# Three of a sort group's eight steps hand three value columns to GpSimd, and the bucket one-hots are made two steps sooner

## The chip, the cores and the metric

The kernel runs on one core of one Trainium2 chip. The metric is the device time of one execution in microseconds; the engines are TensorE (PE in the profile), VectorE (DVE), ScalarE (ACT), GpSimd (POOL) and SyncE (SP). A program is built once and the same inputs are used in every run.

## The reference

A session recommender on a graph. The part that this change concerns is the first line below: 150,000 weighted edges in random order are summed into 12,501 nodes of 128 features, twice.

```python
h = emb; acc = emb                                  # N = 12501 nodes, D = 128
for _ in range(2):
    h = segment_sum(adj_val[:, None] * h[adj_col], adj_row, num_segments=N)
    acc = acc + h
graph_item_embs = acc / 3
combined = graph_item_embs[items] + item_features[items]      # 512 sessions of 50 items
...                                                 # attention over a session, 12 * l2norm -> select
scores = select @ l2norm(graph_item_embs).T         # (512, 12501)
```

## The kernel before

**Stages.** The kernel first counts how many edges fall into each of 49 buckets of 256 rows (to about 88 us of the profile), then sorts all edges by bucket into a table in HBM (to about 737 us), then goes through the sorted edges twice, with one gather by GpSimd for 128 edges at a time (L649), and last computes the sessions and the scores. Only the sort is touched by the change.

**A sort group.** Edges lie as 128 partitions by 1,172 columns. `GR` = 19 groups have `SG` = 8 steps of `C` = 8 columns each; the last has `LAST` = 3 steps. Every edge has a place (partition, column) in a 128 x 72 picture of its group (`LC` = 72). In a step, DVE makes two one-hots from the places: `hot_columns` (L964, bf16, 128 x 576, into one of `Q` = 4 slots of `hot_c`) and `hot_partitions` (L972, f32, 128 x 1024, into one of four slots of `at_p`). Both read the row of candidates from PSUM and the places from SBUF. The one-hot of the columns is then multiplied by each edge's code and by its value, giving `at_c`, 8 columns t of 2 x 72: ACT does columns 0 to `CA` - 1 = 5 with two activations each (L723, in `payloads`), DVE does the last two in one instruction (`last_columns`, L980, 128 x 288). PE multiplies `at_p` by `at_c` column by column (L1550, in `permute`) and sums the group's picture in a PSUM bank. A slot is used again four steps later.

**After a group.** In step 1 of the next group, after two columns of its own, ACT copies the picture out of PSUM (`evacuate`, L709). GpSimd then does a small gate operation (L598), adds the picture's blocks to the sorted table with 9 indirect DMAs that it issues itself (`scatter`, L604), waits for them to land, and frees the buffers with another gate operation (L611). Then it waits for the next group.

**Places of the next group.** Between its one-hots, DVE works out the places of group g + 1 while group g is permuted: `hot_buckets` (L900, 128 x 3136 bf16, the one-hot of the buckets into the single buffer `hot_b`; the first `KEPT` = 7 groups kept theirs from the counting and need none), PE's prefix sums of it (`edges_before`, L1535 on PE, then the reduction L988 on DVE in step 3), a scan over 1,666 elements (`lane_scan`, L1020) in step 4, six folds (L1037, L1045, L1048) in steps 5 to 7, and in step 7 `place_rounded` (L1054), `place_partition` (L1060) and `place_column` (L1065). Each of these waits for the one ahead of it by the semaphore `s_rk`. The first `hot_columns` of group g + 1 waits for the last of them.

**Order.** The order on each engine is written out by hand, and each engine waits for the others by semaphores alone: `hot_columns` waits until ACT is done with the slot, `hot_partitions` until PE is, ACT waits for `hot_columns` and for PE's release of the slot.

```python
for s in range(SG):                     # sort_group on DVE, cut to what matters
    if s == 0 and hot is hot_b:
        hot_buckets(g + 1)
    ...
    hot_columns(g, s, h); hot_partitions(g, s, h)
    ...                                 # the s-th piece of the places of g + 1
    last_columns(g, s)
```

## Time and profile before

| | |
|---|---|
| median of three runs | 3988.06 us (3985.89 to 3988.77) |
| the profiled execution: its time, its span | 3990.2 us, 3988.2 us |
| DVE busy in the span | 3011.5 us (76%) |
| POOL busy | 2657.9 us (67%) |
| PE busy | 2638.1 us (66%) |
| ACT busy | 830.1 us (21%) |
| L980, DVE's multiplication of the last two columns | x147, 97.7 us, 664 ns each |
| L972, DVE's one-hot of the partitions | x147, 178.6 us, 1215 ns each |
| L723, ACT's activations | x1764, 569.7 us, 415 ns each |
| L900, the bucket one-hots | x12, from 295.9 to 660.3 us |

A busy time is the sum of an engine's instructions; where one starts before the last has ended, both are counted in a mean duration, so the step from start to start is shorter than the mean. The whole span has stages with different limits: the shares above say little on the sort, which lies between about 88 and 737 us. The stage behind it begins with GpSimd's first gather (L649).

### The profile page before, as it was taken

The numbers are of one execution on the slowest core, as the hardware profiler recorded it, in microseconds if no ns is written. First come the engines' busy times: TensorE is split into PE (matmuls) and PEld (weight loads), VectorE is DVE, ScalarE is ACT, GpSimd is POOL, SyncE is SP. The second block draws the span as 40 slices with busy tenths as digits, with TensorE's granted clock in tenths as the row PEclk, the third lists the DMA queues.
The fourth block names the chain that finished last, engine by engine and source line by source line (L and its number), as shares of the span: only waits on it lengthen the run. The fifth ranks groups of instructions, "written<-read, shape, count | busy, mean of one in ns | idle before, by whom it ended". The sixth has DMA issues, their size and how long they took to land.

```text
span 3988.2 us, 79764 instructions
## 1 busy us (share of the span) xinstructions
PE 2638.1 (66%) x14097; PEld 2222.1 (56%) x14098; DVE 3011.5 (76%) x7238; ACT 830.1 (21%) x2728; POOL 2657.9 (67%) x2685
## 2 busy tenths in 40 slices
PE   4899889555566566566666556665556555565898
PEld 2676666455565555555555555555555555553454
DVE  8999999767777677777777677767677777677675
ACT  0999999200000000000000000000000000004554
POOL 1355555777777777777776777777777777775771
PEclk7899999777777776777778677778787787786999
DMA  1011111422222222222223222222222222234343
GB/s 37 3 4 3 3 3 3 110 53 54 55 54 54 54 55 55 55 55 55 55 55 103 62 55 55 56 56 56 56 55 55 55 55 55 54 81 140 95 139 139
DMA packets 165449, 228.71 MB, mean 57 GB/s; under 512 B 79020, under 2 KB 119084, under 8 KB 164908
## 3 DMA queue, kind: packets, MB, share of 16 engines
q0 software_dynamic: 102640, 162.39, 19.8%
q1 hardware_dynamic: 47856, 58.94, 4.8%
q10 hardware_dynamic: 14540, 3.70, 0.8%
q14 instruction: 377, 3.09, 0.2%
q8 instruction: 36, 0.59, 0.1%
HBM read 183.57 MB, written 41.35 MB: 56 GB/s over the span
## 4 chain that ended last, share of the span: by engine, by line
DMA 30%; POOL 27%; issue 19%; DVE 13%; PE 6%; ACT 2%; SPq 2%; ACTq 0%; DVEq 0%; POOLq 0%
POOL store L649 25%; DMA store<-in_L_rec_emb,store 16%; DMA store<-table,store 13%; PE bank L1707 2%; DVE store L1020 2%; DVE big L964 2%; PE bank L1650 2%; POOL store L676 1%; DVE store L972 1%; ACT big L723 1%; DVE big L980 1%; DVE big L1445 1%; SPq L496 1%; DVE store L1045 1%; DVE store L906 1%
## 5 line engine op out<-in xcount | busy, mean ns | idle before, releaser
L1650 PE MATMUL bank<-store,shared 128*128 x9792 | 1731.2, 351 | 1137.5 <-POOLq L634 790.5
L1650 PEld LDWEIGHTS bank<-store,shared 128*128 128x128 f32 x9792 | 1610.9, 258 | 1257.8 <-issue 1255.5
L1338 DVE TENSOR_TENSOR acc<-acc,bank 128x256 f32 x2448 | 1022.6, 418 | 799.7 <-PE bank L1650 780.5
L1288 DVE TENSOR_SCALAR shared<-bank,mlo,mval 128x256 f32<-128x256 f32 x2448 | 1324.0, 541 | 0.0
L649 POOL DMA_INDIRECT store<-in_L_rec_emb,store x1128 | 1065.4, 945 | 384.2 <-issue 326.0
L649 POOL DMA_INDIRECT store<-table,store x1128 | 1066.4, 945 | 370.0 <-issue 317.9
L739 ACT COPY mlo<-store 128x24 f32 (+1 forms) x102 | 21.5, 211 | 2793.0 <-PE bank L1650 1977.6
L723 ACT ACTIVATE big<-big 128x72 f32<-128x72 bf16 x1764 | 569.7, 415 | 0.0
L1550 PE MATMUL bank<-big,store 128*128 128x144 f32 x2352 | 480.2, 333 | 72.1 <-DVE store L972 17.3
L1550 PEld LDWEIGHTS bank<-big,store 128*128 128x128 f32 x2352 | 357.0, 206 | 192.8 <-ACT big L723 169.5
L604 POOL DMA_INDIRECT sorted_edges<-moved,block_to x167 | 311.2, 1863 | 57.1 <-issue 57.1
L676 POOL DMA_INDIRECT store<-combined,sidi x200 | 192.3, 962 | 94.4 <-issue 57.3
L972 DVE TENSOR_TENSOR store<-bank,place_p 128x1024 f32<-128x1024 f32 x147 | 178.6, 1215 | 0.0
L598 POOL TENSOR_TENSOR gate<-gate 128x1 f32<-128x1 f32 x19 | 6.2, 326 | 245.9 <-ACT moved L709 245.9
L964 DVE TENSOR_TENSOR big<-bank,place_c 128x576 bf16<-128x576 f32 x147 | 110.3, 750 | 0.3
L1707 PE MATMUL bank<-acc,big 128*128 128x512 f32 (+1 forms) x200 | 96.5, 625 | 2.6 <-DVE big L1493 2.6
L980 DVE TENSOR_TENSOR big<-big 128x288 f32<-128x288 bf16 x147 | 97.7, 664 | 0.0
L1499 DVE COPY store<-bank 128x512 f32<-128x512 f32 x48 | 33.2, 692 | 65.7 <-PE bank L1707 65.7
L1707 PEld LDWEIGHTS bank<-acc,big 128*128 128x128 f32 x200 | 37.0, 198 | 60.5 <-issue 26.4
L1020 DVE TENSOR_TENSOR_SCAN store<-shared,big 128x1666 int16<-128x1666 bf16 x19 | 68.9, 3629 | 0.7
L1696 PEld LDWEIGHTS bank<-w2c,big 128*128 128x128 f32 x400 | 50.6, 191 | 30.6 <-ACT big L841 18.0
L1419 DVE SCALAR_TENSOR_TENSOR big<-store,maskn,big 128x128 f32<-128x128 f32 x192 | 54.9, 346 | 13.0 <-DMA store<-combined,sidi 12.3
(265 smaller groups left out, 1439.4 us busy)
## 6 DMA issues: line engine op xcount, KB each, us to landing
store<-in_L_rec_emb ACTq DMA_DIRECT2D x3008, 0.5 KB
store<-in_L_rec_emb SPq DMA_DIRECT2D x3008, 0.5 KB
store<-table SPq DMA_DIRECT2D x3008, 0.5 KB
store<-table ACTq DMA_DIRECT2D x3008, 0.5 KB
scores<-store SPq DMA_DIRECT2D x48, 512.0 KB, 2.8
store<-in_L_rec_emb,store POOLq DMA_INDIRECT x1128
store<-table,store POOLq DMA_INDIRECT x1128
table<-acc SPq DMA_DIRECT2D x7, 896.0 KB, 10.6
```

The source lines that it names most:

```text
L604: pool.indirect_dma_start(slots, bass.IndirectOffsetOnAxis(block_to[:, h, k:k + 1], 0), moved[:, h, (skip + k) * R:(skip + k + 1) * R, :]. ...
L649: pool.indirect_dma_start(msg[:, j % RING, :], None, source, bass.IndirectOffsetOnAxis(m_col[:, j:j + 1], 0)).then_inc(s_g[gi % (T // GRP4 ...
L676: pool.indirect_dma_start(seq[:, half, l, :], None, combined, bass.IndirectOffsetOnAxis(sidi[:, l, bt:bt + 1], 0)).then_inc(s_sq[half * NG ...
L723: last = act.activation(at_c[:, r, t, q, :], hot_c[:, r, :, t], ACT.Copy, scale=what[:, bass.ds(n * C + t, 1)])
L964: dve.tensor_tensor(hot_c[:, r, :, :], row_c.unsqueeze(2).broadcast_to([P, LC, C]), place_c[:, h, s * C:(s + 1) * C].unsqueeze(1).broadcas ...
L972: dve.tensor_tensor(at_p[:, r, :, :], row_p.unsqueeze(1).broadcast_to([P, C, P]), place_p[:, h, s * C:(s + 1) * C].unsqueeze(2).broadcast_ ...
L1020: dve.tensor_tensor_scan(summed[:, :, :].rearrange("p b t -> p (b t)"), carry[:, :, :].rearrange("p b t -> p (b t)"), pairs[:, :, :].rearr ...
L1288: dve.tensor_scalar(onehot[:, u % SR, :], bank[7][:, 0:BUCKET], mlo[:, u:u + 1], mval[:, u:u + 1], ALU.is_equal, ALU.mult).then_inc(s_S[u ...
L1338: add = dve.tensor_tensor(acc[:, bass.ds(off, BUCKET)], acc[:, bass.ds(off, BUCKET)], bank[u % PR][:, 0:BUCKET], ALU.add)
L1550: last = pe.matmul(group_bank(h)[:, 0:2 * LC], at_p[:, r, t, :], at_c[:, r, t, :, :].rearrange("p w c -> p (w c)"), start=(s == 0 and t == ...
L1650: last = pe.matmul(bank[u % PR][:, q * D:(q + 1) * D], onehot[:, u % SR, q * P:(q + 1) * P], msg_flat[:, bass.ds(offs[u], D)], start=True, ...
L1707: pe.matmul(score_bank(bt, n)[:, 0:w], selT[:, :], acc[:, 512 * n:512 * n + w], start=True, stop=True).then_inc(s_sc, 1)
```

## The change

In the steps s = 0, 1 and 7 of a group (`LENT`), ACT multiplies five columns instead of six, DVE none instead of two, and GpSimd multiplies columns 5 to 7 in one instruction of 128 x 432 elements, with a semaphore of its own (`s_valg`). On GpSimd the instruction for step 7 of group g + 1 stands behind the DMA issues of `scatter(g)` and ahead of the wait for their landing, and those for steps 0 and 1 of group g + 2 behind it. `hot_buckets` for group g + 2 is now made in step 6 of group g, where before it stood in step 0 of group g + 1, and PE's `edges_before` follows it. PE waits for `s_valg` ahead of column 5 of those steps, and DVE waits for it before it writes the same slot of `hot_c` four steps later.

```diff
+            def last_columns(g, s):                       # on GpSimd
+                n, r = SG * g + s, s % Q
+                pool.wait_ge(s_hc, n + 1)
+                pool.wait_ge(s_pm, n + 1)
+                pool.tensor_tensor(at_c[:, r, CL:C, :, :],
+                                   hot_c[:, r, :, CL:C].rearrange("p n t -> p t n").unsqueeze(2).broadcast_to([P, C - CL, 2, LC]),
+                                   pays[:, bass.ds(n * C + CL, C - CL), :].unsqueeze(3).broadcast_to([P, C - CL, 2, LC]),
+                                   ALU.mult).then_inc(s_valg, 1)
...
+                if ahead:
+                    last_columns(g + 1, SG - 1)
                 pool.wait_ge(s_free, g + 3)
                 pool.wait_ge(s_sct, 16 * (NK * g + blocks))
                 pool.tensor_tensor(gate[:, 2:3], gate[:, 1:2], gate[:, 1:2], ALU.add).then_inc(s_free, 1)
+                if ahead:
+                    last_columns(g + 2, 0)
+                    last_columns(g + 2, 1)
...
-                for t in range(CA):
+                own = CL if s in LENT else CA             # ACT: 5 or 6 columns
+                for t in range(own):
...
                 dve.wait_ge(s_val, CA * n + CA)
+                if (s - Q) % SG in LENT:
+                    ge(dve, s_valg, NL * g + (LENT.index((s - Q) % SG) + 1 - (NL if s < Q else 0)))
...
                 for s in range(SG):                       # sort_group on DVE
-                    if s == 0 and hot is hot_b:
-                        hot_buckets(g + 1)
-                    elif s == 3:
+                    if s == 6 and early:
+                        hot_buckets(g + 2)
+                    if s == 3:
...
-                    last_columns(g, s)
+                    if s not in LENT:
+                        last_columns(g, s)
...
                     permute(g, s, h, SG)                  # sort_group on PE
-                    if s == 0:
-                        edges_before(g + 1, hot)
+                    if s == 6 and hot is not None:
+                        edges_before(g + 2, hot)
```

On DVE, at the seam of the groups 16 and 17 (written out behind the loop), the order before runs from step 7's `hot_columns` (L964) over `place_rounded` (L1054) to the `hot_buckets` of group 18 (L900) and steps 0 and 1:

```order
L964 TENSOR_TENSOR big<-bank,place_c 128x576
L972 TENSOR_TENSOR store<-bank,place_p 128x1024
L1054 TENSOR_SCALAR round<-posf 128x64
L980 TENSOR_TENSOR big<-big 128x288
L1060 TENSOR_SCALAR place_p<-round 128x64
L1065 SCALAR_TENSOR_TENSOR place_c<-place_p,posf 128x64
L900 TENSOR_TENSOR store<-shared,big 128x3136
L964 TENSOR_TENSOR big<-bank,place_c 128x576
L972 TENSOR_TENSOR store<-bank,place_p 128x1024
L980 TENSOR_TENSOR big<-big 128x288
L964 TENSOR_TENSOR big<-bank,place_c 128x576
```

At the same seam the changed kernel has this order, with `hot_columns` now at L992, `place_rounded` at L1082, `place_column` at L1093 and `targets` at L1106:

```order
L992 TENSOR_TENSOR big<-bank,place_c 128x576
L1000 TENSOR_TENSOR store<-bank,place_p 128x1024
L1082 TENSOR_SCALAR round<-posf 128x64
L1088 TENSOR_SCALAR place_p<-round 128x64
L1093 SCALAR_TENSOR_TENSOR place_c<-place_p,posf 128x64
L992 TENSOR_TENSOR big<-bank,place_c 128x576
L1000 TENSOR_TENSOR store<-bank,place_p 128x1024
L992 TENSOR_TENSOR big<-bank,place_c 128x576
L1000 TENSOR_TENSOR store<-bank,place_p 128x1024
L1106 TENSOR_TENSOR block_to<-bank,block_id 128x9
```

The multiplications L980 of steps 7, 0 and 1 are gone, and so is the bucket one-hot between `place_column` and the next `hot_columns`; it stands one step earlier, between the second and the third fold:

```order
L1073 TENSOR_TENSOR store<-store 128x768
L926 TENSOR_TENSOR store<-shared,big 128x3136
L1073 TENSOR_TENSOR store<-store 128x384
L992 TENSOR_TENSOR big<-bank,place_c 128x576
L1000 TENSOR_TENSOR store<-bank,place_p 128x1024
```

On GpSimd a group of the changed kernel (the last one that is `ahead`, written out behind the loop) reads as follows; L609 is the multiplication, L602 and L627 the two gates, L618 the scatter's DMAs:

```order
L602 TENSOR_TENSOR gate<-gate 128x1
L618 DMA sorted_edges<-moved,block_to 18816x16 x9
L609 TENSOR_TENSOR big<-big 128x432
L627 TENSOR_TENSOR gate<-gate 128x1
L609 TENSOR_TENSOR big<-big 128x432 x2
L602 TENSOR_TENSOR gate<-gate 128x1
```

Before, nothing stood between a scatter's DMAs and its second gate, nor between that gate and the next group's first.

## Rows read from the trace of the kernel before

**Rows 1.** Busy time by stretch, two sort groups: microseconds, then each engine's.
```profile
core 0: us, PE busy (x) PEld busy (x) DVE busy (x) ACT busy (x) POOL busy (x), PEclk, DMA share, GB/s
239.51:271.82 32.31, 29.36 (x156) 22.04 (x155) 31.05 (x46) 31.34 (x106) 17.40 (x11) 0.95 0.12 3
403.41:436.43 33.02, 29.50 (x152) 22.14 (x151) 32.40 (x48) 31.35 (x106) 18.26 (x11) 0.93 0.12 3
```
**Rows 2.** Who waited for whom, 110 to 304 us: us in total, times, longest.
```profile
ACT idle L717 <- DVE big L964: 7.2, 6, 2.7
DVE ahead L988 <- PE bank L1535: 5.5, 6, 1.0
```
**Rows 3.** Who waited for whom, 337.17 to 668 us.
```profile
ACT idle L717 <- DVE big L964: 16.3, 11, 2.6
```
**Rows 4.** Timeline of DVE, steps 7 and 0: start, us, instruction.
```profile
657.40 0.75 DVE L964 TENSOR_TENSOR big<-bank,place_c 128x576 bf16<-128x576 f32 x1
658.07 1.22 DVE L972 TENSOR_TENSOR store<-bank,place_p 128x1024 f32<-128x1024 f32 x1
659.20 0.18 DVE L1054 TENSOR_SCALAR round<-posf 128x64 f32<-128x64 f32 x1
659.30 0.68 DVE L980 TENSOR_TENSOR big<-big 128x288 f32<-128x288 bf16 x1
659.89 0.19 DVE L1060 TENSOR_SCALAR place_p<-round 128x64 f32<-128x64 f32 x1
660.11 0.22 DVE L1065 SCALAR_TENSOR_TENSOR place_c<-place_p,posf 128x64 bf16<-128x64 f32 x1
660.25 1.78 DVE L900 TENSOR_TENSOR store<-shared,big 128x3136 bf16<-128x3136 bf16 x1
```
**Rows 5.** Timeline of DVE, one group later, at a seam without L900.
```profile
692.95 0.23 DVE L1065 SCALAR_TENSOR_TENSOR place_c<-place_p,posf 128x64 bf16<-128x64 f32 x1
693.26 0.76 DVE L964 TENSOR_TENSOR big<-bank,place_c 128x576 bf16<-128x576 f32 x1
```
**Rows 6.** Timeline of ACT, the last full group: the stall, a step, the last evacuation.
```profile
683.98 0.19 ACT L717 COPY idle<-ones 128x1 f32<-128x1 f32 x1 [1.44 <-DVE big L964]
...
695.90 3.86 ACT L723 ACTIVATE big<-big 128x72 f32<-128x72 bf16 x12
699.67 0.17 ACT L717 COPY idle<-ones 128x1 f32<-128x1 f32 x1
...
701.02 0.26 ACT L709 COPY moved<-bank 128x144 f32<-128x144 f32 x1
```
**Rows 7.** Timeline, places where DVE and POOL instructions meet.
```profile
78.59 0.80 DVE L953 TENSOR_SCALAR big<-big 128x1248 int32<-128x1248 int32 x1
78.75 1.25 POOL L614 IOTA store<- 128x640 f32 x1 [67.52 <-DVE store L951]
79.43 1.23 DVE L954 TENSOR_SCALAR big<-big 128x1248 f32<-128x1248 int32 x1
...
403.35 0.66 DVE L980 TENSOR_TENSOR big<-big 128x288 f32<-128x288 bf16 x1
403.41 0.60 POOL L598 TENSOR_TENSOR gate<-gate 128x1 f32<-128x1 f32 x1 [12.29 <-ACT moved L709]
...
411.55 3.63 DVE L1020 TENSOR_TENSOR_SCAN store<-shared,big 128x1666 int16<-128x1666 bf16 x1
412.31 4.23 POOL L604 DMA_INDIRECT sorted_edges<-moved,block_to  x1 [0.30 <-issue]
```
**Rows 8.** Timeline of POOL at the start: its plain operations by size.
```profile
4.49 0.29 POOL L566 TENSOR_SCALAR_AFFINE_SELECT ident<-ident 128x128 f32<-128x128 f32 x1 [0.16 <-POOL ident L564]
7.42 1.13 POOL L579 IOTA big<- 128x1152 f32 x1
```
**Rows 9.** Timeline of POOL at the end of the sort.
```profile
701.36 0.19 POOL L598 TENSOR_TENSOR gate<-gate 128x1 f32<-128x1 f32 x1 [10.45 <-ACT moved L709]
...
733.46 0.19 POOL L611 TENSOR_TENSOR gate<-gate 128x1 f32<-128x1 f32 x1 [1.45 <-DMA sorted_edges<-moved,block_to]
737.14 1.01 POOL L649 DMA_INDIRECT store<-in_L_rec_emb,store  x1 [3.49 <-DVE store L1267]
```

More of the change, by code:

```diff
@@ L68, in recommender_program @@
     Q = 4
+    CL = CA - 1
+    LENT = (0, 1, SG - 1)
+    NL = len(LENT)
     ECOLS = (GR * SG + Q) * C
@@ L621, in _ @@
             pool.wait_ge(s_zero, 16)
-            with pool.Fori(0, GR // 2) as i:
+            for s in LENT:
+                last_columns(0, s)
+            last_columns(1, 0)
+            last_columns(1, 1)
+            with pool.Fori(0, GR // 2 - 1) as i:
                 for h in range(2):
-                    scatter(2 * i + h, h)
+                    scatter(2 * i + h, h, ahead=True)
+            scatter(GR - 3, 0, ahead=True)
+            scatter(GR - 2, 1)
             scatter(GR - 1, 0, NKL, FIRST)
@@ L724, in payloads @@
                                               scale=what[:, bass.ds(n * C + t, 1)])
-                    last.then_inc(s_val, 1)
+                    last.then_inc(s_val, 1 + CA - own if t == own - 1 else 1)
             with act.Fori(0, GR // 2) as i:
@@ L1078, in targets, with sort_group @@
                 dve.tensor_tensor(block_to[:, h, 0:blocks], bank[7][:, 0:blocks], number[:, :], ALU.add).then_inc(s_to, 1)
-            def sort_group(g, h, width=LC, hot=hot_b):
+            def sort_group(g, h, width=LC, hot=hot_b, early=True):
                 for s in range(SG):
-                    if s == 0 and hot is hot_b:
-                        hot_buckets(g + 1)
-                    elif s == 3:
+                    if s == 6 and early:
+                        hot_buckets(g + 2)
+                    if s == 3:
                         edges_before(g + 1)
@@ L1153, in _ @@
             sort_group(GR - 3, 0)
-            sort_group(GR - 2, 1, LCL)
+            sort_group(GR - 2, 1, LCL, early=False)
             dve.wait_ge(s_lat, 3)
@@ L1159, in _ @@
                 hot_partitions(GR - 1, s, 0)
-                last_columns(GR - 1, s)
+                if s not in LENT:
+                    last_columns(GR - 1, s)
                 if s == 0:
@@ L1544, in permute @@
                 pe.wait_ge(s_hp, n + 1)
+                own = CL if s in LENT else CA
                 for t in range(C):
-                    if t < CA:
+                    if t < own:
                         pe.wait_ge(s_val, Q * CA + CA * n + t + 1)
-                    elif t == CA:
-                        pe.wait_ge(s_valv, n + 1)
+                    elif t == own and s in LENT:
+                        pe.wait_ge(s_valg, NL * g + (LENT.index(s) + 1))
+                    elif t == own:
+                        pe.wait_ge(s_valv, (SG - NL) * g + (s + 1 - sum(x < s for x in LENT)))
                     last = pe.matmul(group_bank(h)[:, 0:2 * LC], at_p[:, r, t, :],
@@ L1567, in _, with sort_group @@
             edges_before(0, kept[:, 0])
[L1569 removed]
+            pe.wait_ge(s_rk, 1)
+            edges_before(1, kept[:, 1])
+            def sort_group(g, h, hot=hot_b):
                 for s in range(SG):
                     permute(g, s, h, SG)
[L1573 to L1574 removed]
+                    if s == 6 and hot is not None:
+                        edges_before(g + 2, hot)
                     elif s == 4:
@@ L1578, in _ @@
             for g in range(KEPT - 1):
-                sort_group(g, g % 2, kept[:, g + 1])
-            with pe.Fori(KEPT // 2, GR // 2) as i:
+                sort_group(g, g % 2, kept[:, g + 2] if g + 2 < KEPT else hot_b)
+            with pe.Fori(KEPT // 2, GR // 2 - 1) as i:
                 for h in range(2):
-                    sort_group(2 * i + h, h, hot_b)
+                    sort_group(2 * i + h, h)
+            sort_group(GR - 3, 0)
+            sort_group(GR - 2, 1, None)
             for s in range(LAST):
```

6 lines of the change are left out of this document (3 added, 3 removed).

## The prediction

> **What bounds the kernel now.** I read the busy times by stretch first, the waits second, the timeline third. A sort group takes 32.3 us early and 33.0 us late; DVE is busy for 31.05 and 32.40 of them, ACT for some 31.35 in both [rows 1]. So two engines are nearly full, and the waits tell which one sets the pace. DVE waits for PE alone, 5.5 us in six early groups, when the prefix sums come late, and for nothing of weight later [rows 2, 3]. ACT waits for DVE once in a group, 16.3 us in eleven waits late [rows 3], 1.44 us in the last full group, where the scan and the first folds hold back step 5's `hot_columns` [rows 6]. A chain through DVE therefore sets the group's time, with ACT some 1.5 us behind, and early on the loop DVE, ACT, PE, DVE adds about 0.9 us. PE is granted 0.93 to 0.95 of its 2.4 GHz here and its weight loads fill 22 of 33 us [rows 1], so it has room. GpSimd is busy for 17 to 18 us and then waits for the next evacuation, up to 12.29 us [rows 1, 7, 9]. The end of the sort hangs on GpSimd: its chain from the last full picture (701.36) to the last gate (733.46) and the first gather (737.14) has fixed length [rows 9]. What the change is worth is how much sooner ACT can evacuate that picture, now at 701.02 [rows 6].
>
> **What is removed.** On DVE, one multiplication is worth its step from start to start, 659.30 to 659.89, 0.59 us [rows 4], not its 0.68. In steps 0 and 1 nothing else changes: 2 x 0.59 = 1.18. In step 7, `place_rounded` was followed after 0.10 us by a multiplication that had no need of it; now `place_partition` follows and must wait for it, which takes 0.22, as between the next two links (659.89 to 660.11) [rows 4]. That leaves 0.69 - 0.22 = 0.47. Together 1.65 us a group, or for groups 0 to 16, 28.0 us, and 1.2 us more in steps 0 and 1 of group 17. From step 5 of group 17 on, ACT is the slower one (its waits stop at 683.98), and there it is its own saving that counts: an activation takes 3.85/12 = 0.32 us [rows 6], and steps 7 and 0 lose two each, 1.3 us. Sum: 30.5 us. Elsewhere ACT's six fewer activations a group (1.9 us) only keep it behind DVE: its work falls to about 29.3, and DVE's to about 31.5 late and 29.7 early. For the early groups I estimate whether a slot can be late: DVE needs some 10 us for any four steps (four times 1.80 for the two one-hots, two or three multiplications, the pieces of the places), while ACT and PE trail by 6 to 9, so none is.
>
> **What is moved.** `hot_buckets` cost 1.71 us of DVE (660.25 to 661.96) wherever it stands. At the seam it also hid the wait of `hot_columns` for `place_column`: without it the step from one to the other is 0.31 us, with it 0.14 [rows 4, 5]. That costs 0.17 in the twelve groups that have it. Between the second and the third fold it hides a wait of the same kind, about 0.13. I put the two at nothing. PE's prefix sums are now made in step 6 for a reduction in step 3 of the next group: the 5.5 us of early waits [rows 2] go altogether. PE has some 3 us of work more between steps 6 and 7 instead of between 0 and 1; the evacuation comes two ACT steps later, so this is covered. On GpSimd the scatter's issues now meet `hot_buckets` in step 6, and one of them will be held as the scan holds one today (4.23 us instead of 1.55) [rows 7]; GpSimd is about 2 us early there and would lose 1.7 of them. The DVE side has a few more semaphore waits, hidden in the queue behind instructions of 0.7 to 1.2 us.
>
> **What is added, and where it collides.** GpSimd's multiplication of 432 elements for each partition stands in no trace. From below: an iota writes 1,152 elements in 1.13 us, 0.98 ns for each, and the operation of one column takes 0.19 [rows 8, 9], so 432 elements take at least 0.6 us. The affine select reads and writes 128 in 0.29 us [rows 8], 0.78 ns for each behind the fixed part. If two inputs and the output were each paid in turn, an element would cost about 0.8 + 0.8 + 1.0 = 2.6 ns and the instruction 1.3 us. From above: DVE itself takes 0.59 us for 288 elements [rows 4], 2 ns each where its plain f32 one-hot takes 1.1, since the columns are picked out of `hot_c` with a stride. Doubling 2.6 in the same way gives 2.4 us. I take 1.4, near the middle sum, with 0.6 and 2.4 as ends. (An estimate apart from the sum: the Trainium skill, GPSIMD Engine Reference, section 3.1, gives about 2.6 cycles of 1.2 GHz an element with two inputs, and section 7 about one more cycle when the step is over 8 bytes. That would be 1.1 and 1.5 us; no row here has such an instruction.)
>
> That time is not on anyone's path as work. PE needs columns 5 to 7 about 3.2 us after `hot_columns`, when ACT is done with its five; GpSimd starts about 0.15 us after `hot_columns` (the gate starts 0.08 after ACT's copy ends at 701.28 [rows 6, 9]). But DVE and GpSimd hold each other up. The rows show both directions [rows 7]: the one-column gate, 0.19 us alone, takes 0.60 and ends at 404.01, with DVE's L980, which reads two tensors in SBUF; an issue starts under the scan and ends 1.4 us after it; and DVE's L954, the same 1,248 elements as L953, takes 1.23 instead of 0.80, since GpSimd's iota runs until 80.00. So the question is which DVE instructions stand beside the multiplications. In steps 0 and 1 they are one-hots and `targets`, which have one operand in PSUM and L972 lasts 1.215 us on the mean of all 147 (table above), most of them beside scatter issues, as in [rows 4], where GpSimd is idle; the first that could be held is the multiplication of step 2, over 2.7 us after the start. In step 7 it is `place_rounded`, SBUF to SBUF, due 1.05 us after `hot_columns` ends (658.15 to 659.20) [rows 4]. GpSimd ends 0.15 + 1.4 = 1.55 after it: DVE is held for 0.5 us, and 0.1 more by GpSimd's gate right behind. 0.6 x 17 groups = 10.2 us given back.
>
> What holds whom is weighed against a rule here. The Trainium skill (SBUF — State Buffer, "Who interferes with whom") says that a DVE instruction with two SBUF inputs contends with GpSimd's reads, one in a two-port mode with all of GpSimd, and one with a single SBUF input outside these modes not at all. By that rule, the gate under L980 agrees (0.60 us), and L954 agrees (1.23). Applied to step 7 it names `place_rounded` or, at the latest, `place_column`, 0.4 us later: the sum would be 0.2 us a group better if only the latter were held. The page says as well that an issue needs only the write side; the scan has two inputs and holds an issue for 2.7 us here, so the measurement decides.
>
> **Sum.** -30.5 - 5.5 + 10.2 = -25.8 us against the profiled execution (3990.2 us; span 3988.2). The median of the plain runs is 2.1 us below that time, so I subtract from it: 3988.1 - 25.8 = **3962 us**.
>
> **The rivals.**
> 1. *No collision.* The multiplication takes up to 0.9 us, or `place_rounded` isn't held. For: GpSimd's plain operations cost 0.98 ns an element [rows 8]. Against: two inputs, a stride, two types. 3988 - 36 = 3952 us.
> 2. *A long multiplication*, 2.4 us, by the stride that costs DVE double. Held for 1.5 + 0.1 us in step 7: 27 us given back, 3979 us.
> 3. *Slower.* GpSimd's multiplication takes over 2.9 us. From 3.0 on, step 7 gives back all the 36 us (2.1 x 17), and from 2.7 on the multiplication of step 1 reaches into step 2, where L980 reads two SBUF tensors and is held as the gate was. At 3.3 us: 2.5 in step 7; step 1's starts late at 4.2 and ends at 7.5, L980 is due at 5.5, 2.0 more; 4.5 x 17 = 77, or 4029 us. Against: 6.6 ns an element is seven times the iota's rate.
> 4. *No change.* The saving is on DVE and ACT, but GpSimd becomes the bound: 17 to 18 us of issues [rows 1], 3.4 of gates and landing, 1.7 of the new hold and three multiplications of 1.4 make 28, and it must also wait for three `hot_columns` in their order. If it reaches step 7's late, PE, the evacuation and the next scatter slip, and 3984 to 3992 us come out, 3988 with the gain just eaten. Against: the sum leaves 3 us a group.
>
> By the rule of two SBUF inputs alone, rival 1 needs a multiplication under 1.3 us.
>
> **How the numbers follow.** Forecast 0.52, rival 1 0.24, rival 2 0.12, rival 3 0.04, rival 4 0.08. The time is the forecast's. The range runs from 3949 (rival 1 with a little over) to 3979 (rival 2), and leaves out rivals 3 and 4 and some of both ends, under 2 in 10. About 0.2% (8 us) is what a measurement can tell from no change. Faster: the first three cases and a bit of rival 4, 0.88. Within 0.2%: 0.07. Slower: 0.05.
>
> **What would show it.** The group falls from 32.3 to about 30.3 us early and from 33.0 to about 32.1 late; the last evacuation stands near 675. GpSimd's 56 multiplications take about 1.4 us. `place_rounded` starts some 1.6 us behind the end of step 7's `hot_columns`, or shows as 0.7 us long. L988 never waits for PE. ACT's wait at step 5 grows to 2 or 3 us. PE shows no wait for GpSimd. The stages behind the sort keep their length. It would be wrong if the multiplication takes 3 us or more, if ACT's wait vanishes, or if GpSimd reaches step 7 after `hot_columns`.

## The result and the profile after

The changed kernel takes 3941.13 us (median of four runs, 3937.11 to 3943.89), the kernel before, run beside it, 3988.01: ratio 0.9882, 95% interval 0.9865 to 0.99. That is 46.9 us less. The forecast was 26 less, and its range ended at 3949. The profiled execution took 3943.89 us, its span is 3942.0.

The first page lines to read are those of the page's groups that the change touches (line, engine, operation, count, then total and mean duration, then the idle time before them).

```profile
L749 ACT ACTIVATE big<-big 128x72 f32<-128x72 bf16 x1652 | 535.4, 413 | 0.0
L1000 DVE TENSOR_TENSOR store<-bank,place_p 128x1024 f32<-128x1024 f32 x147 | 178.5, 1214 | 0.0
L609 POOL TENSOR_TENSOR big<-big 128x432 f32<-128x432 bf16 x56 | 63.2, 1129 | 115.8 <-DVE big L992 115.8
```

ACT has lost 112 activations, DVE's one-hots last as long as before, and GpSimd's new multiplication takes 1.13 us, where 1.4 was taken. It never makes others wait: GpSimd waits for `hot_columns` ahead of 54 of the 56, and no instruction waits for L609.

The busy times of two sort groups, cut from evacuation to evacuation (answering to [rows 1]):

```profile
core 0: us, PE busy (x) PEld busy (x) DVE busy (x) ACT busy (x) POOL busy (x), PEclk, DMA share, GB/s
228.70:258.62 29.92, 27.49 (x157) 21.79 (x155) 29.61 (x45) 29.45 (x101) 19.59 (x14) 0.94 0.13 3
416.58:448.43 31.85, 28.26 (x157) 21.82 (x155) 31.46 (x45) 29.48 (x101) 20.81 (x14) 0.95 0.12 2
```

A group takes 29.9 us early and 31.85 late, 2.4 and 1.2 less than in [rows 1], and DVE is still full. PE's granted clock is as before. From evacuation to evacuation the early groups take 29.7 to 29.9 us and the late ones 31.6 or 31.9 in turn.

Who waited for whom, first from 110 to 304 us, then from 337 to 640 us:

```profile
POOL big L609 <- DVE big L992: 40.5, 16, 24.2
POOL gate L602 <- ACT moved L734: 20.4, 6, 3.7
ACT idle L742 <- DVE big L992: 4.7, 7, 1.7
...
POOL big L609 <- DVE big L992: 43.4, 30, 2.7
POOL gate L602 <- ACT moved L734: 32.4, 10, 3.5
ACT idle L742 <- DVE big L992: 21.6, 19, 1.7
```

DVE's wait for the prefix sums (5.5 us in [rows 2]) is gone. ACT waits for DVE more often than in [rows 3], though never for more than 1.7 us. PE waits for GpSimd nowhere.

The timeline of DVE and then GpSimd in step 7 of one late group, where the two meet (start, duration):

```profile
407.03 0.75 DVE L992 TENSOR_TENSOR big<-bank,place_c 128x576 bf16<-128x576 f32 x1
407.69 1.22 DVE L1000 TENSOR_TENSOR store<-bank,place_p 128x1024 f32<-128x1024 f32 x1
408.82 0.34 DVE L1082 TENSOR_SCALAR round<-posf 128x64 f32<-128x64 f32 x1
409.20 0.20 DVE L1088 TENSOR_SCALAR place_p<-round 128x64 f32<-128x64 f32 x1
409.43 0.23 DVE L1093 SCALAR_TENSOR_TENSOR place_c<-place_p,posf 128x64 bf16<-128x64 f32 x1
410.04 0.76 DVE L992 TENSOR_TENSOR big<-bank,place_c 128x576 bf16<-128x576 f32 x1 [0.39 <-DVE place_c L1093]
...
408.00 1.11 POOL L609 TENSOR_TENSOR big<-big 128x432 f32<-128x432 bf16 x1 [2.67 <-DVE big L992]
409.07 0.19 POOL L627 TENSOR_TENSOR gate<-gate 128x1 f32<-128x1 f32 x1
```

`place_rounded` takes 0.34 us instead of 0.18 [rows 4] and ends at 409.16, just behind the multiplication (409.11). So it is held, by 0.16 us and not 0.6. Its step to `place_partition` is 0.38 us.

The end of the sort, on ACT and then on GpSimd (answering to [rows 6, 9]):

```profile
668.05 0.26 ACT L734 COPY moved<-bank 128x144 f32<-128x144 f32 x1
...
700.38 0.19 POOL L627 TENSOR_TENSOR gate<-gate 128x1 f32<-128x1 f32 x1 [1.44 <-DMA sorted_edges<-moved,block_to]
704.16 1.01 POOL L674 DMA_INDIRECT store<-in_L_rec_emb,store  x1 [3.60 <-DVE store L1297]
```

The last full picture is evacuated 32.97 us sooner (701.02 to 668.05), the first gather starts 32.98 sooner (737.14 to 704.16). The sort thus gained 33.0 us between these two traces, and the other 13 came from behind it. (One group of the trace of before takes 34.0 us where its neighbours take 33.1. In the nine kernels below that have the sort of before, unchanged, the last full picture is evacuated at 699.05 to 700.13, and in the five with the changed sort at 667.53 to 668.06. So 31 to 33 us is the sort's gain, and about 1 us of the 33.0 is this trace's own.) There the gathers themselves are summed up by the trace: how many there are, when the first and the last of a layer started, and what GpSimd waited for ahead of them, in us and times. First the kernel before, then the changed one:

```profile
L649 POOL DMA_INDIRECT store<-in_L_rec_emb,store x1128: 938/944/1200, 737.1 to 2182.3; - x188
L649 POOL DMA_INDIRECT store<-table,store x1128: 938/944/1182, 2197.3 to 3618.7; - x188
...
  DMA store<-in_L_rec_emb,store: 49.9, 86
  DMA store<-table,store: 33.8, 82
```

```profile
L674 POOL DMA_INDIRECT store<-in_L_rec_emb,store x1128: 938/944/1302, 704.2 to 2139.7; - x188
L674 POOL DMA_INDIRECT store<-table,store x1128: 938/944/1227, 2154.6 to 3569.0; - x188
...
  DMA store<-in_L_rec_emb,store: 40.0, 81
  DMA store<-table,store: 24.8, 69
```

The same 2,256 gathers take 1445.2 and 1421.4 us from the first to the last before, 1435.5 and 1414.4 after: 9.7 and 7.0 us less, in code that the change doesn't touch. A gather takes 944 ns in both. What shrinks most between these two traces is GpSimd's wait for earlier gathers to land, by 9.9 and 9.0 us. What lies behind the start of the last session gather takes 3.9 us more (86.7 against 82.8); the other traces of this document, in which the same code runs, have 83.0 to 88.0 there, so that is no effect of the change. So there are two questions: whether the 33 us came as predicted, and where the other 13 came from.

### The profile page after: what moved, and what is told of

It reads as the page before. It is cut to its first block, busy times and chain, and to the rows that moved or that the text cites. A ratio compares the mean times of both kernels' runs of the same rounds, so it can differ in the third digit from the quotient of the medians.

```text
span 3942.0 us, 79662 instructions
## 1 busy us (share of the span) xinstructions
PE 2631.9 (67%) x14097; PEld 2235.5 (57%) x14098; DVE 2984.7 (76%) x7182; ACT 795.0 (20%) x2616; POOL 2717.6 (69%) x2741
## 4 chain that ended last, share of the span: by engine, by line
POOL 30%; DMA 26%; issue 20%; DVE 13%; PE 7%; ACT 2%; SPq 1%; DVEq 0%; ACTq 0%; POOLq 0%
POOL store L674 28%; DMA store<-in_L_rec_emb,store 15%; DMA store<-table,store 10%; PE bank L1744 2%; PE bank L1687 2%; DVE store L1000 2%; ACT big L749 2%; DVE store L1048 1%; DVE big L992 1%; POOL store L701 1%; DVE store L1073 1%; DVE big L1475 1%; DVE big L1008 1%; PE bank L1708 1%; DVE store L932 1%
## 5 line engine op out<-in xcount | busy, mean ns | idle before, releaser
L749 ACT ACTIVATE big<-big 128x72 f32<-128x72 bf16 x1652 | 535.4, 413 | 0.0
L1583 PE MATMUL bank<-big,store 128*128 128x144 f32 x2352 | 452.9, 330 | 65.4 <-DVE store L1000 20.1
L618 POOL DMA_INDIRECT sorted_edges<-moved,block_to x167 | 311.1, 1863 | 59.3 <-issue 59.3
L609 POOL TENSOR_TENSOR big<-big 128x432 f32<-128x432 bf16 x56 | 63.2, 1129 | 115.8 <-DVE big L992 115.8
L992 DVE TENSOR_TENSOR big<-bank,place_c 128x576 bf16<-128x576 f32 x147 | 110.3, 750 | 2.9 <-DVE place_c L1093 1.8
L1733 PEld LDWEIGHTS bank<-w2c,big 128*128 128x128 f32 x400 | 51.7, 194 | 31.2 <-ACT big L867 17.5
L843 ACT ACTIVATE big<-bank,posb 128x128 f32<-128x128 f32 x200 | 58.3, 393 | 15.2 <-PE bank L1715 14.8
```

Of the source, the lines that this page charges most:

```text
L618: pool.indirect_dma_start(slots, bass.IndirectOffsetOnAxis(block_to[:, h, k:k + 1], 0), moved[:, h, (skip + k) * R:(skip + k + 1) * R, :]. ...
L749: last = act.activation(at_c[:, r, t, q, :], hot_c[:, r, :, t], ACT.Copy, scale=what[:, bass.ds(n * C + t, 1)])
L992: dve.tensor_tensor(hot_c[:, r, :, :], row_c.unsqueeze(2).broadcast_to([P, LC, C]), place_c[:, h, s * C:(s + 1) * C].unsqueeze(1).broadcas ...
L1583: last = pe.matmul(group_bank(h)[:, 0:2 * LC], at_p[:, r, t, :], at_c[:, r, t, :, :].rearrange("p w c -> p (w c)"), start=(s == 0 and t == ...
```

## The experiments

All times below are medians, each beside runs of the kernel before (whose medians are 3987.6 to 3989.2 us). "Last evacuation" is that of the last full picture, and a layer's length is from its first to its last gather.

### The halves of the change

**sooner**: only the one-hots and prefix sums are made sooner.

```diff
-    LENT = (0, 1, SG - 1)
+    LENT = ()
```

> Only the second half of the change: the bucket one-hots two steps sooner, PE's prefix sums with them, and no multiplication on GpSimd (DVE and ACT have all columns, as before). Theory A (the sort is DVE's chain, and early groups also lost 0.9 us to the late prefix sums): early groups fall from 32.3 to 31.4 us, late ones stay at 33.0 to 33.1, the sort ends 5 to 6 us sooner, at about 731 us for GpSimd's first gather. Rival B (the sooner one-hots are what most of the 33 us of the sort came from, because ACT's and PE's lag is what counts): 15 us or more. For the gather stages behind the sort (1445 us and 1421 us from first to last gather before, 1436 and 1414 in the changed kernel): if their shortening is caused by the multiplication on GpSimd, they stay at 1445 and 1421 here.

**lent**: only the multiplications are lent to GpSimd, with `hot_buckets` and `edges_before` in their old place.

```diff
-                    if s == 6 and early:
-                        hot_buckets(g + 2)
+                    if s == 0 and hot is hot_b:
+                        hot_buckets(g + 1)
```

> Only the first half of the change: GpSimd multiplies columns 5 to 7 in steps 0, 1 and 7, while the bucket one-hots stand where they stood before. Theory A: DVE loses 1.65 us a group and is held for 0.16 us by the multiplication of 1.13 us, so the late groups fall by about 1.5 us to 31.5; the early ones still wait for the prefix sums, or do so less since ACT's step 0 is shorter; the sort ends 26 to 28 us sooner, the first gather stands near 710. Rival B: if most of the gain was the sooner one-hots, 15 us or less. The gather stages: 1436 and 1414 us if the multiplication is what shortens them, 1445 and 1421 if it is the sooner one-hots.

| | median us | ratio, 95% | last evacuation | groups early, late | layers |
|---|---|---|---|---|---|
| sooner | 3966.76 | 0.9941 (0.9927 to 0.9955) | 693.77 | 31.2, 33.1 | 1435.2, 1414.6 |
| lent | 3954.74 | 0.9916 (0.9898 to 0.9934) | 679.68 | 31.3, 31.9 | 1435.3, 1414.4 |

In the sort, `sooner` is worth 7.2 us and `lent` 21.3, together 28.6 of the 33.0, by the trace of before; by the other nine with its sort each of the three is about 1.3 us less, so `sooner` is at the 5 to 6 us that were expected. `lent` stays behind the 26 to 28 us that were expected of it: the early groups still take 31.3 us, and the late ones 31.9 on the mean, not 31.5. Of the 4.4 us (5.7 by the other nine) that only come of having both, 3.2 can be read: with the multiplications alone, DVE runs into the prefix sums harder, as the waits from 110 to 304 us show (5.5 us in [rows 2]):

```profile
ACT idle L742 <- DVE big L992: 12.1, 7, 3.3
DVE ahead L1016 <- PE bank L1565: 8.7, 6, 1.6
```

So the sooner one-hots take 8.7 us of waits away once GpSimd helps, and 5.5 when it doesn't. That the gather stages lost the same 17 us in both halves, although neither half shares a moved instruction with the other, was the first hint: both kernels have in common only the new semaphore `s_valg`, which `sooner` declares and never uses.

### The hold in step 7

**no_seven**: step 7 goes back to DVE and ACT.

```diff
-    LENT = (0, 1, SG - 1)
+    LENT = (0, 1)
```

> The changed kernel, but step 7's multiplications are back with DVE and ACT; GpSimd has those of steps 0 and 1 alone. Theory A: DVE loses 0.47 - 0.16 (hold) - the rest of the seam = about 0.3 us a group less gain than with step 7 on GpSimd if DVE alone counts, so the late groups take 32.0 to 32.1 us instead of 31.74, the early ones 30.0 to 30.1 instead of 29.7, and the whole 5 to 7 us more: 3946 to 3948. If the hold in step 7 were as dear as I had forecast (0.6 us), step 7 would bring nothing, and the time would stay at 3941 or fall.

**four**: GpSimd multiplies four columns instead of three, so its instruction has 576 elements.

```diff
-    CL = CA - 1
+    CL = CA - 2
```

> The changed kernel with four columns on GpSimd in the three steps instead of three (128 x 576, by the 2.2 ns an element of the measured 1.125 us about 1.45 us long); ACT keeps four. Theory A (the sort is bound by DVE, and GpSimd holds place_rounded for as long as the multiplication outlasts hot_partitions): DVE is held for 0.16 + 0.33 = about 0.5 us in step 7, the group takes 0.3 us more, 3946 us. Rival (ACT's chain sets the pace by now): ACT loses 1.9 us a group more, and the time falls.

`no_seven` took 3942.08 us (0.9886, 0.9871 to 0.9902), `four` 3945.33 (0.9893, 0.9878 to 0.9908). The changed kernel's sort is 5.2 and 4.2 us shorter than theirs (last evacuations at 673.28 and 672.22). For `four` the medians say the same, 4.2. For `no_seven` they differ by 0.95 us alone, where 5 to 7 were expected: its layers are 1433.8 and 1411.8 us, 4.3 us less together than those of the changed kernel, for no reason that these runs show. By the expectation's own words, a time that stays at 3941 would have meant a hold of 0.6 us; so the whole time can't decide here, and the steps of DVE must. In `no_seven` `place_rounded` is followed by the multiplication again:

```profile
411.01 0.18 DVE L1080 TENSOR_SCALAR round<-posf 128x64 f32<-128x64 f32 x1
411.11 0.68 DVE L1006 TENSOR_TENSOR big<-big 128x288 f32<-128x288 bf16 x1
411.70 0.18 DVE L1086 TENSOR_SCALAR place_p<-round 128x64 f32<-128x64 f32 x1
```

That is 0.69 us from `place_rounded` to `place_partition`, against 0.38 in the changed kernel: 0.31 us a group, or 5.3 in 17, and the sort is 5.2 us longer. In `four`, DVE and then GpSimd:

```profile
411.65 0.65 DVE L1082 TENSOR_SCALAR round<-posf 128x64 f32<-128x64 f32 x1
412.33 0.20 DVE L1088 TENSOR_SCALAR place_p<-round 128x64 f32<-128x64 f32 x1
...
410.81 1.44 POOL L609 TENSOR_TENSOR big<-big 128x576 f32<-128x576 bf16 x1 [2.66 <-DVE big L992]
412.20 0.20 POOL L627 TENSOR_TENSOR gate<-gate 128x1 f32<-128x1 f32 x1
```

GpSimd's instruction is 0.31 us longer (median 1440 ns against 1125), and `place_rounded` lasts 0.31 longer, again ending just behind it (412.30 and 412.25). The hold is thus shown to be there, with a dose and a response. In 18 groups of the changed kernel and 18 of `four`, `place_rounded` starts with 0.15 to 0.61 us of the multiplication left, and ends 0.05 or 0.06 us behind it in every one. GpSimd's gate, which runs on for 0.1 us behind that, adds nothing. By the hold alone, 17 groups would cost 5.3 us, and the sort of `four` is 4.2 longer. ACT's waits for DVE from 337 to 640 us grew from 21.6 to 43.3 us in `four`: relieving ACT of a fourth column bought 1 us at most, since it was not ACT that set the pace.

### A delay ahead of the gathers

The first theory on the 13 us was a matter of time: the table of sorted edges is ready 33 us sooner, so GpSimd's gathers meet the row reads of ScalarE's and SyncE's queues in another phase. If so, a delay ahead of the first gather must change a layer's length too.

**before_late, after_late**: GpSimd makes 60 additions (some 28 us) between the last gate of the sort and the first gather. They count up a semaphore of their own, `s_late`, which is named ahead of most others.

```diff
+            with pool.Fori(0, 6) as i:
+                for k in range(10):
+                    pool.wait_ge(s_late, 10 * i + (k + 1))
+                    pool.tensor_tensor(moved[:, 0, :, :], moved[:, 1, :, :], moved[:, 1, :, :], ALU.add).then_inc(s_late, 1)
```

> The kernel before with the same delay of some 30 us on GpSimd ahead of the first gather. Theory C: the gather stages change from 1445 and 1421 us, by up to 10 us each. Rival D: they stay within 2 us, and the time is before plus the delay. Rival E: they move by up to 10 us either way.

> The changed kernel, with GpSimd kept busy between the sort's last gate and the first gather: a loop of 60 additions of 128 x 144 elements on a buffer that is free by then, each waiting for the one ahead, 30 us or so (its length is read from the trace). Theory C (the gather stages are shorter by 17 us for a reason that lies in when they start, against the clock's throttling or against the stages of other engines): the stages go back to 1445 and 1421 us, and the time is the changed kernel's plus the delay plus 13. Rival D (they are shorter whatever the moment, by the program's own layout or by chance of a run): they stay near 1436 and 1414, and the time is the changed kernel's plus the delay. Rival E (the lengths vary by 10 us from kernel to kernel with no rule): neither.

**before_tiny**: the same with two additions instead of 60.

> The kernel before with the delay loop of the late variant cut down to one turn of two additions, about 1 us instead of 28: the same additional semaphore (named behind s_gate) and the same place, nearly no delay. If the shorter first gather stage of the late variant (1414 instead of 1445 us) came from the delay, since ScalarE's and SyncE's row reads get ahead of GpSimd's gathers: the stage is 1435 to 1446 us here, the time 3980 to 3990. If it came from the semaphore or the code's place: about 1414 us with 28 us less of delay, so 3953 us.

**before_sem**: the kernel before, with one semaphore that nothing uses.

```diff
         s_valv = sem("s_valv")
+        s_valg = sem("s_valg")
```

> The kernel before with one more semaphore, named at the place where the changed kernel names s_valg, and used by nothing; every semaphore named behind it moves by one. Theory F (the gather stages are 1435 and 1414 us in the changed kernel and in both of its halves, to 0.2 us, and 1445 and 1421 before; what the three have in common and the kernel before has not is that semaphore): 1435 and 1414 us here too, and about 13 us less than before. Rival (the order of the instructions in the sort, or the moment at which the sort ends, sets them): nothing changes, 3988 us.

| | median us | ratio, 95% | first gather | layers |
|---|---|---|---|---|
| before_late | 3981.71 | 0.9983 (0.9975 to 0.9992) | 765.9 | 1414.1, 1411.6 |
| after_late | 3938.69 | 0.9873 (0.9857 to 0.9889) | 732.4 | 1409.1, 1409.4 |
| before_tiny | 3971.76 | 0.996 (0.9947 to 0.9974) | 735.4 | 1435.7, 1413.7 |
| before_sem | 3973.34 | 0.9965 (0.9951 to 0.9979) | 735.5 | 1435.1, 1412.9 |

`before_late` by itself would have seemed to bear out the theory of the phase, with a layer 31 us shorter; the theory falls by the last two lines. One unused semaphore takes 15.6 us off the kernel before (3988.99 beside it), and its layers have the changed kernel's lengths to 1.5 us:

```profile
L650 POOL DMA_INDIRECT store<-in_L_rec_emb,store x1128: 939/945/1355, 735.5 to 2170.6; - x188
L650 POOL DMA_INDIRECT store<-table,store x1128: 940/945/1205, 2185.4 to 3598.3; - x188
```

`before_tiny`, which has another new semaphore and no delay to speak of, does the same. The delay itself has a price of its own, worked out between kernels with as many new semaphores: 3981.71 - 3971.76 = 10.0 us for a first gather 30.5 us later. (`after_late`, where `s_late` and `s_valg` move most others by two as in `after_two` below, says the same: 3938.69 - 3928.9 = 9.8 us for 28.3 us.) So when GpSimd alone is late at this point, two thirds come back in layer 1, whose waits for landed gathers fall from 42.6 to 28.5 us.

### Which semaphore

A semaphore's number follows from its place in the list of names, so `s_valg`, named in the middle, moves every one behind it by one. The next runs move parts of the list. All but the first are the kernel before with one unused semaphore, named at different places.

**valg_last**: the changed kernel with `s_valg` named behind all others, so that the rest keep the numbers of the kernel before.

```diff
-        s_valg = sem("s_valg")
         s_pm = sem("s_pm")
...
+        s_valg = sem("s_valg")
```

> The changed kernel, word for word, except that its new semaphore s_valg is named behind all others, so that every other semaphore keeps the number it has in the kernel before. Theory F (numbering the semaphores one higher is worth some 15 us in the stages behind the sort, and the rest of the change 33 us in the sort): the first gather at 704 as in the changed kernel, gather stages back at 1445 and 1421 us, 3955 to 3957 us in all, inside the range that I had forecast. Rival (the changed kernel's gain behind the sort has another source as well): 3941 us.

**sem_last, sem_at_g, sem_past_g, sem_at_mtr, sem_at_line**: the unused one named last, ahead of `s_g` (the gathers), behind `s_g`, ahead of `s_mtr`, and ahead of `s_line` (the diff is that of the last).

```diff
+        s_none = sem("s_none")
         s_line = [sem(f"s_line{h}") for h in range(4)]
```

> The kernel before with one unused semaphore named behind all others: one more semaphore, no number moved. If the numbers matter: 3988 us, stages 1445 and 1421. If one more semaphore as such does it (at the start or end of the program): 3973 us.

> The kernel before with one unused semaphore named just ahead of s_g, the six that the gathers count up when they land; s_line, the four of the row reads, and all ahead of them keep their numbers, s_g and all behind move by one. If the numbers of s_g or of those behind it matter: 3973 us, stages 1435 and 1414. If those of s_line, or of the sort's own semaphores matter: 3988 us.

> The kernel before with one unused semaphore named just behind s_g: only s_gd, s_S, s_mm, s_acc and those behind move, no semaphore that a gather or a row read counts up. If it is the landing of gathers that the numbers speed up: 3988 us here. If it is the hand-over between PE, DVE and GpSimd (s_gd, s_S, s_mm, s_acc): 3973 us.

> The kernel before with one unused semaphore just ahead of s_mtr: the sort's own semaphores (s_pm, s_sct, s_free and so on) keep their numbers; those of the stage between sort and gathers (s_mtr to s_lines), s_line, s_g and all behind move by one. 3973 us if the cause is s_line or a semaphore from s_mtr to s_lines; 3988 us if it is one of the sort's.

> The kernel before with one unused semaphore just ahead of s_line, the four that the row reads of ScalarE and SyncE count up: s_line and all behind it move by one, nothing ahead. If it is the numbers of s_line (alone or with s_g, which alone did nothing): 3973 us, gather stages 1435 and 1414. If not: 3988 us, and the cause lies with semaphores named between s_valv and s_lines.

| | median us | ratio, 95% | layers |
|---|---|---|---|
| valg_last | 3955.81 | 0.9915 (0.9902 to 0.9929) | 1443.4, 1422.0 |
| sem_last | 3990.04 | 1.0001 (0.9992 to 1.0011) | 1444.2, 1420.9 |
| sem_past_g | 3988.6 | 0.9996 (0.9987 to 1.0005) | 1444.3, 1422.7 |
| sem_at_g | 3989.76 | 1.0003 (0.9994 to 1.0012) | 1444.2, 1421.6 |
| sem_at_line | 3972.53 | 0.996 (0.9947 to 0.9974) | 1435.0, 1412.3 |
| sem_at_mtr | 3971.99 | 0.9959 (0.9945 to 0.9973) | 1435.6, 1413.5 |

With the numbers put back, the changed kernel takes 3955.81 us, 33.4 less than before beside it (3989.16), which is the sort's gain. The rest follows the numbers. Moving `s_g` and what is named behind it does nothing; moving `s_line` as well is worth the whole. Among the traces with equal numbers of `s_line` and no delay, a layer's length repeats within 3 us (1443.4 to 1445.2 and 1420.9 to 1422.7 unmoved, 1433.8 to 1435.7 and 1411.8 to 1414.6 by one), so the two sets don't overlap. `s_line` are four semaphores that the row reads of a step count up, 128 for each, issued by ScalarE's and SyncE's queues. In `valg_last` GpSimd waits for earlier gathers again:

```profile
L674 POOL DMA_INDIRECT store<-in_L_rec_emb,store x1128: 939/947/1371, 703.7 to 2147.1; - x188
L674 POOL DMA_INDIRECT store<-table,store x1128: 941/947/1182, 2161.2 to 3583.2; - x188
...
  DMA store<-in_L_rec_emb,store: 41.7, 77
  DMA store<-table,store: 28.1, 70
```

Its waits are only 1.7 and 3.3 us longer than those of the changed kernel, though its layers are 7.9 and 7.6 longer; the gaps between a gather and the next issue (653.1 us in all, against 645.5) and the gathers (947 ns) have part of it. The waits themselves scatter as much: `sem_last` has 43.4 and 28.2, the kernel before 49.9 and 33.8, with layers of one length to 1 us. So the wait for landing is one place where the time may show, not the only one.

### More steps of the numbers

**sem_two**: the kernel before with two unused semaphores. **after_two, after_three, after_four**: the changed kernel with one, two and three, which stand right behind `s_valg` (not ahead of it, as two of the expectations have it); all that is named behind them moves by two, three and four against the kernel before.

> The kernel before with two unused semaphores behind s_valv, so that everything behind moves by two. If what counts is one bad number that some semaphore had: 3973 us, as with one. If it is odd against even, or the place in a small group of numbers: back to 3988 us, or another step further down, to some 3960.

> The changed kernel with one unused semaphore more ahead of s_valg, so that everything behind moves by two against the kernel before. 3941 us if one step is all there is to have; near 3925 if the steps add; 3956 if it is odd against even. This is also the try for a version that beats the changed kernel.

> The changed kernel with two unused semaphores named ahead of s_valg, so the numbers of the semaphores behind it stand three above those of the kernel before (the change itself: one; the run with one unused: two). No instruction is added. Theory A, each step of the numbers of s_line takes time off the gather stages, first step 15.6 us, second about 10: a third step takes off up to 10 more, 3919 to 3925 us. Theory B, the numbers count only by some grouping (even and odd, or blocks of four), and the step just past is as good as it gets: 3929 us or back above it, up to 3955. By both, the sort's length is that of the changed kernel, with the first gather near 704 us.

> The same with three unused semaphores, numbers four above those of the kernel before. Theory A: as much again or a little less, 3910 to 3922 us. Theory B with blocks of four: all four s_line semaphores stand as before within their block, and the time goes back to that without any step, near 3955 us as with s_valg named last. First gather near 704 us by both.

| steps of the numbers | kernel before | changed kernel | layers of the changed kernel |
|---|---|---|---|
| 0 | 3990.04 (sem_last) | 3955.81 (valg_last) | 1443.4, 1422.0 |
| 1 | 3973.34 (before_sem) | 3941.13 (the change itself) | 1435.5, 1414.4 |
| 2 | 3962.66 (sem_two) | 3928.9 (after_two) | 1428.1, 1410.0 |
| 3 | not run | 3936.59 (after_three) | 1434.1, 1411.7 |
| 4 | not run | 3948.09 (after_four) | 1439.8, 1418.6 |

Both columns fall alike, and the difference between them, 32.2 to 34.2 us, is the sort's gain at every step. The steps don't add without end, as one theory had it: the third takes 7.7 us back, the fourth 11.5 more. Nor does the fourth give the time of no step, as blocks of four would have it: 3948 is 7.7 us below 3956. `after_two` is the best version measured, 3928.9 us, a ratio of 0.9852 (0.9837 to 0.9867) to the kernel before and 12 us below the changed kernel, with no instruction more.

## Why the prediction was wrong

**The step that failed** is "The stages behind the sort keep their length". They did not, because the change names a new semaphore in the middle of the list and so moves the numbers of `s_line`. That is worth 14.7 us between `valg_last` and the changed kernel, and 15.6 between the kernel before and `before_sem`. Without it the changed kernel takes 3955.81 us, inside the range of 3949 to 3979. Nothing in the trace of before shows such a term; what was known ahead is that the change has a semaphore more. So the range would have held for the change as a rearrangement of work, 6 us below the forecast.

**The mis-sized term** is the hold, "0.6 x 17 groups = 10.2 us given back". It is 0.16 us for each group, 0.38 from `place_rounded` to `place_partition` where 0.22 was unhindered, so 2.7 us (step by step, the 17 add up to 2.6: 0.02 in the first, 0.29 in two, 0.13 to 0.16 in the others). The sum would have been -30.5 - 5.5 + 2.7 = -33.3, and the sort measured -31 to -33. The 0.44 us between 0.6 and 0.16 have three parts. GpSimd has 0.29 us left when `place_rounded` starts, not 0.5 (the multiplication is 0.27 shorter, but starts 0.07 later behind `hot_columns`). The gate's 0.1 didn't come: DVE's instruction ends at 409.16, while the gate still runs. And the prediction let the 0.18 us of `place_rounded` begin only when GpSimd was done, while 0.13 of them pass during the hold, since it ends 0.05 behind the multiplication. The rows had this already [rows 7]: L954 ends 0.66 us behind the iota (80.66 and 80.00), though the same elements took L953 0.80. That DVE is held in step 7 was right, as `four` shows, though not how the hold adds up.

**The multiplication.** The ends of 0.6 and 2.4 us held, and the stride brought no doubling. The sum of two inputs and an output gave 1.3 us, which was too high by 0.17 already, and 1.4 was a choice above it. With 432 elements in 1125 ns and 576 in 1440, an element takes 2.19 ns and 0.18 us are fixed, which is the 0.19 of GpSimd's one-column operation [rows 9]. The Trainium skill (GPSIMD Engine Reference, section 3.1) gives about 2.6 cycles of 1.2 GHz, 2.17 ns, and the trace agrees; its section 7 adds about a cycle an element for a step over 8 bytes, and these runs show none, though the columns are picked out of `hot_c` with a step of 16 bytes.

**What holds whom.** The prediction weighed whether `place_rounded` or only `place_column` would be held. It is `place_rounded` (0.34 us, 0.65 in `four`), while `place_column` takes 0.23 in all of them. This instruction with a single SBUF input is thus held until GpSimd's multiplication ends. The Trainium skill (SBUF — State Buffer, "Who interferes with whom") says that of DVE's operations a tensor_scalar is among those that can enter a two-port mode, and that whoever comes second is then blocked for the whole of the other's instruction; the two lengths, 0.34 and 0.65 us, agree with that, though no run here shows the mode itself.

**The other terms.** Early, L1016 (L988 before) never waits for PE: right, and `lent` shows that the move took 8.7 us and not 5.5, since DVE had become faster. The removal in step 7 was taken as 0.47 us before the hold, and with the hold of 0.16 `no_seven` gives 0.31: right. The seam that lost `hot_buckets` costs 0.37 or some 0.6 us in turn from `place_column` to `hot_columns`, where it was 0.15 or some 0.6 with `hot_buckets` behind it, 0.12 a group on the mean of twelve, or 1.5 us in all. Between the folds `hot_buckets` gives 0.12 back (2.17 us from the second fold to the third, 1.70 of them its own, where the step was 0.58), so "I put the two at nothing" was right. It holds a scatter's issue too, as forecast, by 0.85 us and not 1.7: the issue that starts at 402.95, beside L926 below, takes 2.38 us. DVE and then ACT in that group:

```profile
402.11 1.79 DVE L926 TENSOR_TENSOR store<-shared,big 128x3136 bf16<-128x3136 bf16 x1
404.87 0.19 ACT L742 COPY idle<-ones 128x1 f32<-128x1 f32 x1 [1.67 <-DVE big L992]
```

Groups: 29.8 and 31.7 us, where 30.3 and 32.1 were forecast, both 0.4 or 0.5 too high by the hold. The last evacuation was forecast at 675 and stands at 668.05.

**Wrong in a mark, without weight.** ACT's wait "grows to 2 or 3 us": it comes more often (21.6 us in 19 waits against 16.3 in eleven) and stays at 1.7 at most. At step 5, where the mark looked for it, it fell to 0.45 to 0.77 us late. The new wait, 1.66 to 1.68 us, stands in step 6, where the 1.70 us of `hot_buckets` are now ahead of `hot_columns` (second line above).

**The rivals.** Rival 1 ("no collision", 3952 us) came nearest in time among those of the sort, and is not what happened: there is a collision, a small one. Rival 2 and rival 3 fall by the 1.13 us. Rival 4 falls: GpSimd waits for `hot_columns` ahead of nearly every multiplication, 43.4 us in 30 waits late.

## What stays open

Why the numbers of the four `s_line` semaphores matter isn't settled. Shown is that moving the four by one, with all named behind them, makes the layers 7 to 10 us shorter each, and that moving only what is named behind them does nothing. The second to fourth step moved everything from the middle of the list on; the time falls for two steps and rises for the next two, and that this too is due to `s_line` is likely, but not shown. Not told apart is whether it is the number of each one, which of the four share something, or their place against other semaphores that are counted up at the same time. A run that moves `s_line` alone, with all others in place, wasn't made. Nor is it shown why a GpSimd that starts late catches up two thirds in layer 1, or why the layers of `no_seven` are 4.3 us shorter than those of the changed kernel.

## What to carry to other kernels

When an edit adds a semaphore, name it behind all others first, or time it against a twin that has the semaphore and nothing else: here 15 us of a 47 us gain came from a line that does nothing, and the twin told it in one run. When stages that a change doesn't touch change their length, compare their sums in both traces ahead of any story on the touched stage. Where two engines hold each other up as here, cost the overlap by the end of the longer instruction: the short one ended 0.05 us behind it, and what followed on the other engine added nothing. When a small change of the whole time is to prove something of one stage, read the stage in the trace: in `no_seven` 4 of 5 us were hidden by a stage that nobody touched.

## What the runs showed of the hardware

- The numbers of the semaphores that the row reads of ScalarE's and SyncE's queues count up change the length of a stage with 2,256 gathers: 3972.5 us where these and all behind them are moved by one (`sem_at_line`), 3989.8 where only those behind are (`sem_at_g`). With all from the middle of the list moved by zero to four, the changed kernel takes 3955.8, 3941.1, 3928.9, 3936.6 and 3948.1 us.
- A GpSimd multiplication with two SBUF inputs, bf16 by f32 to f32, takes 0.18 us and 2.19 ns for each element of a partition (1125 ns for 432, 1440 for 576), with an input in steps of 16 bytes.
- A DVE instruction of 0.18 us with one SBUF input, started 0.29 us ahead of the end of such a multiplication, ends 0.05 us behind it (0.34 us; 0.65 when the end is 0.60 us away).
- GpSimd's issue of an indirect DMA takes 2.38 to 2.44 us instead of 1.55 when a DVE instruction with two SBUF inputs (bf16, 1.79 us) runs beside it, and ends 1.4 us behind that; under the scan, 4.23 [rows 7].
